# Attention with its rows renumbered, 2 KB pieces of the distance scores, and the row minimum subtracted by GpSimd and ScalarE

## What is computed

```python
scores = jnp.einsum('bhqd,bhkd->bhqk', q, k)
rel_q = jnp.einsum('bhld,lrd->bhlr', q, pos_emb)
rel_k = jnp.einsum('bhrd,lrd->bhlr', k, pos_emb)
scores = (scores + rel_q + rel_k) / jnp.sqrt(jnp.asarray(D, scores.dtype))
probs = jax.nn.softmax(scores, axis=-1)
ctx = jnp.einsum('bhqk,bhkd->bhqd', probs, v)
```

## Time and profile before

| | us |
|---|---|
| median of three runs | 3471.21 (3469.12 to 3471.73) |
| profiled execution, time | 3457.64 |
| profiled execution, span on the core | 3455.9 |
| busy: PE, DVE, ACT, POOL | 2734.2, 2293.6, 1760.5, 986.2 |
| granted PE clock, mean | 0.836 |

### The profile page before, as it was taken

The page is one execution under the profiler, slowest core; times in us unless marked ns, Lnnn a source line. Parts: engine busy times, 40 slices in busy tenths (PEclk is TensorE's granted clock), DMA queues, the critical chain, the costliest instruction groups (busy, mean ns, idle before and its releaser), DMA issues. The chain is left out here.

```text
span 3455.9 us, 68386 instructions
## 1 busy us (share of the span) xinstructions
PE 2734.2 (79%) x18124; PEld 1908.8 (55%) x18124; DVE 2293.6 (66%) x6133; ACT 1760.5 (51%) x3509; POOL 986.2 (29%) x795
## 2 busy tenths in 40 slices
PE   4676478788788788497788888888779498888887
PEld 2344478777787778365455555555446244444443
DVE  5665256555565566397778888888779466666664
ACT  2334345455455455297778888888779111111111
POOL 2333233332332333111112121222111233333344
PEclk7888567777677777599889999999989699999999
DMA  3999799899999999999999999999999301111110
GB/s 108 222 224 213 174 361 341 310 362 332 322 352 346 330 360 367 285 289 263 261 273 272 276 271 268 269 270 261 258 268 296 112 33 64 64 64 64 64 64 20
DMA packets 905515, 807.89 MB, mean 234 GB/s; under 512 B 236808, under 2 KB 809536, under 8 KB 870832
## 3 DMA queue, kind: packets, MB, share of 16 engines
q1 hardware_dynamic: 840112, 640.95, 62.2%
q0 software_dynamic: 29440, 98.07, 12.9%
q10 hardware_dynamic: 35840, 67.12, 7.7%
HBM read 465.93 MB, written 340.05 MB: 233 GB/s over the span
## 5 line engine op out<-in xcount | busy, mean ns | idle before, releaser
L729 DVE TENSOR_TENSOR d_r<-d_pq,d_r 128x1024 f32<-128x1024 f32 x512 | 620.6, 1224 | 461.0 <-PE d_pq L656 315.2
L1069 ACT ACTIVATE t_e<-t_neg,t_low 128x512 f32<-128x512 f32 x1024 | 737.4, 732 | 232.8 <-DVE t_low L1011 226.6
L704 ACT ACTIVATE d_r<-d_pk 128x1024 f32<-128x1024 f32 x512 | 520.6, 1029 | 541.4 <-PE d_pk L669 513.0
L1011 DVE CUSTOM_DVE_ANT_0 t_neg<-t_ps,t_r 128x512 f32<-128x512 f32 x1024 | 671.6, 687 | 25.9 <-issue 25.8
L937 PE MATMUL t_pt<-t_ident,t_e 128*128 128x128 f32 x4096 | 639.1, 279 | 1.1 <-DVE t_eT L1019 0.6
L656 PE MATMUL d_pq<-d_win,d_q 96*128 96x128 bf16 x4096 | 501.7, 287 | 117.4 <-POOL d_q L608 60.6
L927 PE MATMUL t_ps<-t_kb,t_qa 96*128 (+1 forms) x1024 | 402.6, 394 | 235.1 <-DVE t_low L1011 196.6
L937 PEld LDWEIGHTS t_pt<-t_ident,t_e 128*128 128x128 f32 x4096 | 515.2, 144 | 108.1 <-ACT t_eT L1076 13.1
L669 PE MATMUL d_pk<-d_win,d_k 96*128 96x128 bf16 x4096 | 478.5, 276 | 111.7 <-POOL d_k L608 60.4
L656 PEld LDWEIGHTS d_pq<-d_win,d_q 96*128 96x128 bf16 x4096 | 440.1, 189 | 149.5 <-POOL d_q L608 66.5
L669 PEld LDWEIGHTS d_pk<-d_win,d_k 96*128 96x128 bf16 x4096 | 431.0, 192 | 127.4 <-ACT d_r L704 61.3
(11 more groups left out here) (134 smaller groups left out, 2552.8 us busy)
## 6 DMA issues: line engine op xcount, KB each, us to landing
r_scratch<-d_r SPq DMA_DIRECT2D x256, 1024.0 KB, 8.4
t_r<-r_scratch SPq DMA_DIRECT2D x1024, 256.0 KB, 5.3
d_q<-q_chunks_scratch ACTq DMA_DIRECT2D x64, 512.0 KB, 8.6
d_q<-q_chunks_scratch ACTq DMA_DIRECT2D x128, 256.0 KB, 11.5
t_kb<-k_chunks_scratch POOLq DMA_DIRECT2D x32, 512.0 KB, 20.3
q_chunks_scratch<-a_part SPq DMA_DIRECT2D x96, 128.0 KB, 3.5
q_rows_scratch<-a_part SPq DMA_DIRECT2D x96, 128.0 KB, 2.2
k_chunks_scratch<-a_part SPq DMA_DIRECT2D x96, 128.0 KB, 3.5
```

The lines of the kernel that those rows point to most:

```text
L704: nc.scalar.activation(r[lc % 2][:, :, n * KR:(n + 1) * KR], pk[n % 2][:].rearrange("p r l -> p l r"), ACT.Copy).then_inc(k_out, 1)
L729: nc.vector.tensor_tensor(part, pq[n % 2][:], part, ALU.add).then_inc(q_added, 1)
L1011: nc.vector.tensor_tensor_reduce(out=neg[:, L, :], in0=p_s[bank(j, L)][:], in1=r[:, j % RR, L].rearrange("p c r -> p (c r)"), scale=-0.25, ...
L1069: nc.scalar.activation(e[:, j % 2, L, :], neg[:, L, :], ACT.Exp, bias=low[:, j % 2, L:L + 1], scale=-1.0, accum_out=total[:, j // GH, L, j ...
```

## The change

- r in DRAM is laid out so that for each key tile and head the 512 query rows lie together, 256 KB, with a pitch of 260 KB. A read takes one such block, in 128 pieces of 2 KB: partition p gets query rows 4p to 4p + 3. Tile t of a head is now the rows 4p + t, so the score's stationary operand takes every fourth column of q. `experts` numbers its tokens the same way (pieces of 4 KB).
- A head's four reads are issued together, when the head four before is used up. DVE waits for all four before the first tile.
- The exponential moves behind the transposes. DVE still adds and takes the minimum. POOL subtracts the minimum in place in tiles 0 and 1, ACT in tiles 2 and 3, with the other sign. PE transposes two tiles into a double bank, and ACT takes the exponential of 1024 columns at a time out of PSUM straight into `eT`. The copies out of PSUM by DVE and ACT go, and with them the row sums in ACT's accumulator.
- The row sums come from the product: v is copied by POOL into `vx` beside 16 columns of ones. ACT empties the product (`cs`), PE transposes it, DVE inverts the sums, POOL widens them, PE transposes that, and DVE scales. This runs up to two groups behind.
- Scores have two PSUM banks in place of three and run one tile ahead. `neg` has a ring of two heads.
- Batch loads move from POOL's queue to ACT's, one batch ahead, issued after the first head of the batch before. Context stores move from POOL's queue to SP's.

```diff
-RPITCH = TB * TB + 1024
+RPITCH = NT * TB * TB + 1024
...
-            to = r_d[g][tile % NT, tile // NT, :, p * part * TB:(p + 1) * part * TB]
+            to = r_d[g][tile // NT, :, bass.ds(tile % NT * TB * TB + p * part * TB, part * TB)]
...
-        AHEAD = 2
-        BANKS = 3
+        RING = 2
...
+        vx = sb("t_vx", [P, 2, GH, TT, 2, D])
+        r = sb("t_r", [P, RR, NT, TT, TB])
+        neg = sb("t_neg", [P, RING, TT, S])
+        low = sb("t_low", [P, RING, TT])
+        cs = sb("t_cs", [P, 2, S])
+        p_s = [ps(f"t_ps{i}", [P, S]) for i in range(2)]
+        p_t = [ps(f"t_pt{i}", [P, 2, TT, P]) for i in range(2)]
...
+    def subtract(n, j, t):
+        pool.wait_ge(added, TT * n + t + 1)
+        nc.gpsimd.tensor_scalar(neg[:, j % RING, t, :], neg[:, j % RING, t, :],
+                                low[:, j % RING, t:t + 1], None, ALU.subtract).then_inc(pool_sub, 1)
+    def copy_v(step, k):
+        G = 2 * step + k
+        pool.wait_ge(v_loaded[k], 16 * (step + 1))
+        later(pool, weighed, TT * (G - 1))
+        nc.gpsimd.tensor_copy(vx[:, k, :, :, 0, :], vv[:, k]).then_inc(v_copied, 1)
+    def widen(G):
+        pool.wait_ge(inverted, G + 1)
+        later(pool, spread, G)
+        nc.gpsimd.tensor_copy(wide[:], inv[:].rearrange("p t j -> p (t j)").unsqueeze(2)
+                              .to_broadcast([P, GT, CT])).then_inc(widened, 1)
+    def head(step, j):
+        n = U * step + j
+        fixed = isinstance(n, int)
+        if not fixed or n < NH:
+            for t in range(2):
+                subtract(n, j, t)
+        if j % GH == 1 and (not fixed or 2 * GH <= n):
+            widen(2 * step + j // GH - 2)
+        if j % GH == 1 and (not fixed or n < NH):
+            copy_v(step, j // GH)
...
+    def load_r(g, n, j):
+        later(sp, added, TT * (n - RR + 1))
+        for c in range(NT):
+            src = r_d[g][c, n - g * P, 0:NT * TB * TB].rearrange("(p x) -> p x", x=TT * TB)
+            sp.dma_start(r[:, j % RR, c].rearrange("p t r -> p (t r)"), src).then_inc(r_loaded[j % RR], 16)
+    def load_v(b, k):
+        G = BG * b + k
+        later(sp, v_copied, G - 1)
+        sp.dma_start(vv[:, k % 2].rearrange("p h t d -> p (h t d)"),
+                     v_d[b, :, k * GH:(k + 1) * GH].rearrange("p h t d -> p (h t d)")
+                     ).then_inc(v_loaded[k % 2], 16)
+    def store(b, k):
+        sp.wait_ge(scaled, BG * b + k + 1)
+        for j in range(GH):
+            row = (GH * k + j) * D
+            sp.dma_start(cT_d[b, row:row + D, :], out[j * CT:j * CT + D, k % 2, :]
+                         ).then_inc(ctx_stored[k % 2], 16)
+    def batch(g, pair, u):
+        b = 2 * pair + u
+        fixed = isinstance(b, int)
+        for j in range(H):
+            load_r(g, H * b + j, j)
+            k = j // GH
+            if j % GH == 0:
+                load_v(b, k)
+            if j % GH == GH - 1 and (not fixed or BG * b + k >= 3):
+                store(b + (k - 3) // BG, (k - 3) % BG)
...
+    def score(n, j, t):
+        later(pe, added, TT * n + t - 1)
+        lhs = qa[:, 0, n % SLOTS, :].rearrange("r (p t) -> r t p", t=TT)[:, t, :]
+        nc.tensor.matmul(p_s[t % 2][:], lhs, kb[:, :, n % SLOTS, :],
+                         start=True, stop=True).then_inc(scored, 1)
+    def turn(n, j, t):
+        if t < 2:
+            pe.wait_ge(pool_sub, 2 * n + t + 1)
+        else:
+            pe.wait_ge(act_sub, 2 * n + t - 1)
+        if t % 2 == 0:
+            later(pe, exped, 2 * n + t // 2 - 1)
+        for c in range(TT):
+            last = nc.tensor.transpose(p_t[t // 2][:, t % 2, c, :],
+                                       neg[:, j % RING, t, c * P:(c + 1) * P], ident[:])
+        last.then_inc(turned, 1)
+    def weigh(G, par, c):
+        if c == 0:
+            pe.wait_ge(exped, 2 * GH * (G + 1))
+            pe.wait_ge(v_copied, G + 1)
+            later(pe, emptied, G)
+        for j in range(GH):
+            last = nc.tensor.matmul(p_c[j * CT:(j + 1) * CT, :],
+                                    vx[:, par, j, c].rearrange("p o d -> p (o d)"),
+                                    eT[:, par, j, c].rearrange("p t q -> p (t q)"),
+                                    start=(c == 0), stop=(c == TT - 1))
+        last.then_inc(weighed, 1)
+    def sums(G, par):
+        pe.wait_ge(emptied, G + 1)
+        later(pe, scaled, G)
+        for t in range(TT):
+            last = nc.tensor.transpose(p_i[:, t * P:(t + 1) * P], cs[:, par, t * P:(t + 1) * P], ident[:])
+        last.then_inc(summed, 1)
+    def widen(G):
+        pe.wait_ge(widened, G + 1)
+        for t in range(TT):
+            last = nc.tensor.transpose(p_i[:, t * P:(t + 1) * P],
+                                       wide[:, t * GH:(t + 1) * GH, :].rearrange("p j w -> p (j w)"), ident[:])
+        last.then_inc(spread, 1)
+    def head(step, j):
+        n = U * step + j
+        fixed = isinstance(n, int)
+        for t in range(TT):
+            k = TT * j + t
+            nxt = n + (t + 1) // TT
+            if not fixed or nxt < NH:
+                score(nxt, j + (t + 1) // TT, (t + 1) % TT)
+            if not fixed or 1 <= n <= NH:
+                turn(n - 1, j - 1, t)
+            G = 2 * step + k // GT - 1
+            if k % GT in (6, 10, 14) and (not fixed or 0 <= G < NGR):
+                weigh(G, (k // GT - 1) % 2, (k % GT - 6) // 4)
+            G = 2 * step + k // GT - 2
+            if k % GT == 2 and (not fixed or 0 <= G < NGR):
+                weigh(G, k // GT % 2, TT - 1)
+            if k % GT == 4 and (not fixed or 0 <= G < NGR):
+                sums(G, k // GT % 2)
+            if k % GT == 9 and (not fixed or 0 <= G < NGR):
+                widen(G)
...
+    def add(n, j, t, step):
+        dve.wait_ge(scored, TT * n + t + 1)
+        if t == 0:
+            dve.wait_ge(r_loaded[j % RR], HEAD * (2 * step + j // RR + 1))
+        later(dve, turned, TT * (n - RING) + t + 1)
+        nc.vector.memset(tiny[:, t:t + 1], 0.0)
+        nc.vector.tensor_tensor_reduce(out=neg[:, j % RING, t, :].rearrange("p (c r) -> p c r", r=TB),
+                                       in0=p_s[t % 2][:].rearrange("p (c r) -> p c r", r=TB),
+                                       in1=r[:, j % RR, :, t, :], scale=-0.25,
+                                       scalar=3.0e38, op0=ALU.add, op1=ALU.min,
+                                       accum_out=low[:, j % RING, t:t + 1]).then_inc(added, 1)
+    def invert(G):
+        dve.wait_ge(summed, G + 1)
+        sums = p_i[:].rearrange("p (t j w) -> p t j w", j=GH, w=CT)[:, :, :, D]
+        nc.vector.reciprocal(inv[:], sums).then_inc(inverted, 1)
+    def scale(G, par, stores):
+        dve.wait_ge(spread, G + 1)
+        later(dve, ctx_stored[par], STORE * stores)
+        nc.vector.tensor_tensor(out[:, par, :], cs[:, par, :], p_i[:], ALU.mult).then_inc(scaled, 1)
+    def head(step, j):
+        n = U * step + j
+        fixed = isinstance(n, int)
+        for t in range(TT):
+            k = TT * j + t
+            if not fixed or n < NH:
+                add(n, j, t, step)
+            G = 2 * step + k // GT - 2
+            if k % GT == 5 and (not fixed or 0 <= G < NGR):
+                invert(G)
+            if k % GT == 11 and (not fixed or 0 <= G < NGR):
+                scale(G, k // GT % 2, step - 1)
...
+    def subtract(n, j, t):
+        act.wait_ge(added, TT * n + t + 1)
+        nc.scalar.activation(neg[:, j % RING, t, :], neg[:, j % RING, t, :], ACT.Identity,
+                             bias=low[:, j % RING, t:t + 1], scale=-1.0).then_inc(act_sub, 1)
+    def exp(n, j, half, G):
+        act.wait_ge(turned, TT * n + 2 * half + 2)
+        if j % GH == 0 and half == 0:
+            later(act, weighed, TT * (G - 1))
+        to = eT[:, j // GH % 2, j % GH, :, 2 * half:2 * half + 2, :].rearrange("p c t q -> p t c q")
+        nc.scalar.activation(to, p_t[half][:], ACT.Exp, scale=(1.0 if half else -1.0)).then_inc(exped, 1)
+    def empty(G, par):
+        act.wait_ge(weighed, TT * (G + 1))
+        later(act, scaled, G - 1)
+        nc.scalar.activation(cs[:, par, :], p_c[:], ACT.Copy).then_inc(emptied, 1)
+    def head(step, j):
+        n = U * step + j
+        fixed = isinstance(n, int)
+        if not fixed or n < NH:
+            subtract(n, j, 2)
+        if not fixed or 1 <= n <= NH:
+            exp(n - 1, (j - 1) % U, 1, 2 * step + (j - 1) // GH)
+        if not fixed or n < NH:
+            subtract(n, j, 3)
+            exp(n, j, 0, 2 * step + j // GH)
+        if j % GH == GH - 1 and (not fixed or 7 <= n):
+            empty(2 * step + j // GH - 1, (j // GH - 1) % 2)
+    def load(b):
+        u = b % 2
         g, b8 = b // GB, b % GB
         for tensor, src, runs in ((qa, qf_d, A_RUNS), (kb, ks_d, B_RUNS)):
             for row, stored, rows in runs:
+                act.dma_start(tensor[row:row + rows, :, bass.ds(u * H, H), :].rearrange("r n h w -> r n (h w)"),
```

(41 more changed lines are left out.)

284 lines of the change are left out of this document (50 added, 234 removed).

## The result

The changed kernel takes 3430.55 us (median of 4 runs, 3428.93 to 3440.7), the kernel before 3471.47 beside it: ratio 0.989, 95% interval 0.987 to 0.991. That is 41 us less, where 157 were forecast. The profiled execution of after takes 3440.7 us with a span of 3439.0 and is the slowest of its runs. All ratios here compare undisturbed executions: one of e2, 9841.9 us long at a granted clock of 0.235, is left out of its ratio.

What follows compares the result with a forecast made beforehand. DVE was taken to set the head's 3.90 us, with loads stalling 15.9 us each; PE next. Last add 1463 + 998 + 14 x 5 = 2531, with experts 157 less: 3300.6, plus 13.6 gives 3314; range 3235 to 3440.

Steps and rivals of the forecast that it cites:

- A load costs 5 us: Attention: each of 14 batch loads of q and k stalls compute 5 us after the change; bounds 0 and 15.9.
- The load lasts 23.3 us: Attention: 18.6 us for the load's own packets plus 4.7 us for the r packets passing beside them.
- The cover, 4.6 x 3.9 = 17.9 us: Attention: work DVE has during a load, three heads landed ahead plus 1.6 arriving, at 3.9 us each.
- the 1.6 heads: Attention: r arriving during a load, 818 packets of 2 KB, 1.68 MB.
- ACT's share 1 us: Attention: part of the 5 us stall due to ACT's seven DMA issues, 2.9 us in one piece, about two thirds covered.
- Head 3.90 us: Attention: PE's sum of 3.84 us a head, with small waits 3.90, as before; 256 heads take 998 us.
- GpSimd 1.04 us a subtraction: Attention: each of GpSimd's two subtractions a head takes 1.04 us, bounds 0.46 and 1.55; 2.5 us a head in all.
- Start 1463: Attention's effective start after the change, in us, against 1467 before; bounds 1450 and 1475.
- The median: Whole kernel: 13.6 us added to 3300.6, since the earlier kernel's median lay that far above its profiled execution.
- No stall: Rival, attention: loads cost nothing and PE sets everything, 70 us less, 3244; chance 0.20.
- starved as before: Rival, attention: loads starve r as before the change, 153 us more than forecast, 3467, no change; chance 0.09.
- The bandwidth rule of the Trainium skill: Attention's DMA traffic: about 358 GB/s a core makes a batch 68.6 us, a loss of 6.2 in place of 5.

Runs made afterwards that it cites:

- e2: Changed kernel, but from batch 2 on each of the seven load DMAs moves only 64 columns of one head: 3292.7 us, ratio 0.949.
- e1: Changed kernel without the q and k loads of all batches but the first two: 3271.2 us, ratio 0.943.
- e11: Changed kernel with q's three load issues from GpSimd and only k's four from ACT, in one burst: 3439.7 us, ratio 0.992.
- e6: Changed kernel with the same q and k bytes in seven loads, but from other rows and into 128 partitions: 3339.6 us, ratio 0.964.
- e5: Kernel before with only the change's layout of r, its four reads a head and its token order: 3450.3 us, ratio 0.996.
- e10: e5 with PE's wait for the next batch's q and k moved to one head before use: 3454.7 us, ratio 0.997.
- e13: e10 with q landing in pieces of 2 KB in place of 16 KB: 3463.9 us, ratio 0.999.
- e4: Changed kernel with r landing in pieces of 512 B, in a padded buffer: 3532.9 us, ratio 1.021.
- e9: Kernel before with PE's wait for the next batch moved from eight heads to one head before use: 3458.9 us, ratio 0.997.

## Why the prediction was wrong in size

Direction and kind were right, and 3430.6 lies in the range of 3235 to 3440; the gain was forecast at four times its size. By its own steps, at the last add (2531 forecast, 2670.6 measured):

- **A load costs 5 us: the step that failed.** It costs 11.8, 14 x 6.8 = 95 us of the 140. The mis-sized term is the load's length, "The load lasts 23.3 us". From ACT's first issue to the last landing the 14 loads take 27.8 us on average (26.5 to 28.7). The queues over the whole second load, 1549.35 to 1577.66 us:

```profile
q10 hardware_dynamic: 976, 3.15, 57.6%
q1 hardware_dynamic: 1685, 2.94, 43.8%
```

  The load's own packets take 0.576 x 28.3 = 16.3 us (18.6 forecast), those of SP's queue 0.438 x 28.3 = 12.4 us, where 4.7 were forecast. 1.7 of them pass for each of the load's, not 1.21, and one takes 12.4 x 16 / 1685 = 0.12 us, not 0.09. The load isn't 676 packets either: 96 of 16 KB, 768 of 2 KB, and 112 of 4 bytes.
- **The cover, 4.6 x 3.9 = 17.9 us,** was right as a sum, by luck in its parts. By the landing times two heads are there when a load starts and the third lands 1.4 to 3.8 us later (in 13 of 14 loads), so the three heads held. Of the 1.6 heads that were to pass beside the load only one comes in time, since a head counts only when it is whole: the first behind the load is whole at 22.9 us (mean of 14), the second at 28.7, and DVE begins each 0.1 to 0.5 us later (but for one load, which found fewer heads there). Until then DVE has 1.4 us left of its head and four heads, 16.1 us by e1's row: 17.5 us of work in 28.7, which leaves 11.2 of the 11.8. SP's queue brought 2.94 MB in the second load, 2.6 heads of 1.115 MB, more than the forecast's 1.6; but that lengthened the load, and a part of it lay in heads that weren't whole. A deeper ring wasn't tried.
- **ACT's share 1 us.** ACT stands 5 us (1.38 + 3.48), not 7 x 0.42 = 2.9; with few bytes the seven take 3.3 (e2: 1.38 + 1.90), so the load's bytes make them half as long again. That the share lies hidden in r's stall was right for the total. The stalls are seen one behind the other, at heads 2 and 4, but the end is set by the second head behind the load, whole at 28.7 us: with ACT standing 2.7 us the total stays (e11), and only where r comes early does ACT's standing show in full (e6, 5.2 us).
- **Head 3.90 us.** It is 4.03: 256 x 0.13 = 33 us. PE bound it, as forecast, but the product was taken from its own first weight load. From score to score a tile with a product takes 1.75 us in both kernels (first before, then after), 1.09 more than 0.66 and not 0.98:

```profile
2632.28 0.38 PE L927 MATMUL t_ps<-t_kb,t_qa 96*128 x1
...
2634.03 0.39 PE L927 MATMUL t_ps<-t_kb,t_qa 96*128 x1
```

```profile
2618.43 0.38 PE L937 MATMUL t_ps<-t_kb,t_qa 96*128 96x512 bf16 x1
...
2620.18 0.41 PE L937 MATMUL t_ps<-t_kb,t_qa 96*128 96x512 bf16 x1
```

  So a head sums to 2.64 + 1.09 + 0.22 = 3.95. Before it was 2.64 + 1.09 + 0.11 = 3.84 of 3.90: PE was as near to the limit as DVE, and unloading DVE had to be worth nothing. The strided weight load of the score and the two banks cost at most the 0.08 that are left.
- **GpSimd 1.04 us a subtraction.** It took 1.57, just above the upper bound, and was not the limit: 33.42 of 40 us busy.

```profile
L847 POOL TENSOR_SCALAR t_neg<-t_neg,t_low 128x512 f32<-128x512 f32 x465 | 722.8, 1566 | 325.9 <-DVE t_low L1029 325.8
L1029 DVE CUSTOM_DVE_ANT_1 t_neg<-t_ps,t_r 128x512 f32<-128x512 f32 x929 | 619.7, 688 | 198.9 <-issue 198.5
```

- **Start 1463.** By the same count it is 2670.6 - 256 x 4.03 - 14 x 11.8 = 1474, the last 11 us of the 140. The distance stage's last add came at 1430.8 (before 1422.1); in e5, with the same new pitch, at 1419.3, so that part is scatter and the pitch costs nothing. The rest, from the last add to the end of the execution, was forecast at 769.6 us and took 770.1.
- **The median.** 13.6 us were added for the profiled execution of before; that of after lay 10.2 above its own median. By luck that hides 24 of the 140 us. The range held by little: its upper end allows loads of 10 us, and they took 11.8.
- **The rivals.** "No stall" would have needed e1's 64.4 us; "starved as before" is nearer to the truth than its 0.09 said (76.2 us against 78.3), and e10 and e13 bear out its core, that r may starve whatever the packets are. The layout alone, with its larger packets, is worth 1.8 us a batch in the old order of work (e5), the packet size 6.7 in the new (e4). The bandwidth rule of the Trainium skill ("DMA: Bandwidth & Descriptors", Where 436 GB/s comes from: about 358 GB/s for a core) gave 68.6 us a batch, nearer than my sum, for a wrong reason: after moves 390 GB/s at 1580 us and e6 388 in a load.
- **Missed altogether:** that the kernel before waits for a batch eight heads early, and that the change moves this to one. It was worth nothing by itself (e9: 0.997 of before), but it is why e5 looked like a wait for k.

## What to carry to other kernels

A large load that must pass beside a steady stream costs what the DMA engines cannot do in its time. Add up the time that the packets of both take, here 55 us of r and 16.5 of the load in a batch of 64.4, and spread the load over the whole of it. Here spreading (with q in 2 KB pieces) brought 114 us on top of the change's 41, while other issuers or smaller pieces of q in one burst brought nothing. To know whether a ring covers a load, don't count bytes: ask when the first block that is issued behind the load's start is whole. When two waits end together, an edit that removes one shows nothing, and a profile that names one has not cleared the other.
